# Attention core rebuilt: a 32x32 chunk recurrence, a half-size inversion, other batch groups, and a mixture summed on TensorE

## The reference, cut to what matters

```python
attn = where(strict_lower, -(kb @ k.T), 0)        # 32x32 per chunk, kb = k * beta
T = inv(eye - attn);  u = T @ (v * beta);  w = T @ kb
for each chunk:                                    # S is 32x32
    u_i = u - w @ S
    o_i = q @ S + where(lower, q @ k.T, 0) @ u_i
    S = S + k.T @ u_i
```

## Time and profile before

| | |
|---|---|
| median of 3 runs | 506.85 us (506.24 to 511.7) |
| the profiled execution | 506.55 us, of which the span of its instructions is 504.8 us |
| PE busy | 400.6 us (79%), 2822 matmuls, 2822 weight loads |
| DVE, ACT, POOL busy | 343.4 us (68%), 311.7 us (62%), 43.1 us (9%) |
| mean granted TensorE clock | 0.874 of full speed |
| DMA queue of instruction refills (q8) | 34 packets, 0.56 MB |

### The profile page before, as it was taken

How to read it: one execution, slowest core, us unless ns; L and a number is a source line. 1 busy time by engine, 2 the same in 40 slices (tenths; PEclk the granted TensorE clock), 3 DMA queues, 4 the chain that set the end, 5 groups by cost and what they waited for, 6 DMA issues and landing times. The chain is left out here.

```text
span 504.8 us, 7248 instructions
## 1 busy us (share of the span) xinstructions
PE 400.6 (79%) x2822; PEld 290.1 (57%) x2822; DVE 343.4 (68%) x532; ACT 311.7 (62%) x471; POOL 43.1 (9%) x44
## 2 busy tenths in 40 slices
PE   5469998999889958898279999729523298899994
PEld 2346775678667647787146766615201286576783
DVE  2893479747138569999956866694986987487532
ACT  4866886797465757875246646373334179668862
POOL 3000000000000001000400000000719500000000
PEclk9789999999999976799759978658958599999998
DMA  8700007300000000015600000000000000001001
GB/s 281 245 3 1 3 0 213 82 3 0 1 1 1 0 3 1 3 45 148 224 6 2 1 1 1 1 1 0 0 0 1 0 3 1 1 0 45 3 1 42
DMA packets 13484, 17.24 MB, mean 34 GB/s; under 512 B 896, under 2 KB 9088, under 8 KB 13440
## 3 DMA queue, kind: packets, MB, share of 16 engines
q1 hardware_dynamic: 13296, 16.58, 10.7%
q10 hardware_dynamic: 144, 0.01, 0.0%
HBM read 15.55 MB, written 1.05 MB: 33 GB/s over the span
## 5 line engine op out<-in xcount | busy, mean ns | idle before, releaser
L711 PE MATMUL ps_a<-acts,w_f 128*128 128x512 f32 x256 | 104.5, 408 | 1.4 <-DVE acts L1093 0.9
L712 PE MATMUL ps_a<-acts,w_f 128*128 128x512 f32 x256 | 101.4, 396 | 0.0
L711 PEld LDWEIGHTS ps_a<-acts,w_f 128*128 128x128 f32 x256 | 49.1, 192 | 15.2 <-ACT acts L573 1.7
L712 PEld LDWEIGHTS ps_a<-acts,w_f 128*128 128x128 f32 x256 | 49.1, 192 | 11.5 <-issue 1.4
L573 ACT ACTIVATE acts<-ps_a,vec 128x512 fp32r<-128x512 f32 x64 | 44.5, 695 | 0.0
L846 PE MATMUL ps_a<-xnp,conv_w 128*128 128x512 f32 x156 | 38.1, 402 | 0.0
L1112 DVE TENSOR_TENSOR acts<-ghbuf,acts 128x512 fp32r<-128x512 f32 x32 | 21.6, 690 | 23.4 <-ACT acts L573 23.1
L1112 DVE TENSOR_TENSOR acts<-gbuf,acts 128x512 fp32r<-128x512 f32 x32 | 21.7, 690 | 22.3 <-ACT acts L573 22.3
L711 PE MATMUL ps_a<-xn,w_f 128*128 128x512 f32 x32 | 15.0, 470 | 25.3 <-DVE ln L1001 22.2
L846 PEld LDWEIGHTS ps_a<-xnp,conv_w 128*128 128x128 f32 x156 | 29.3, 188 | 8.2 <-issue 1.4
L755 PE MATMUL ps_a<-arena 128*128 128x32 f32 x128 | 17.7, 296 | 12.4 <-ACT arena L482 12.4
(11 more groups left out here) (202 smaller groups left out, 855.2 us busy)
## 6 DMA issues: line engine op xcount, KB each, us to landing
toep<-in_fir SPq DMA_DIRECT2D x16, 288.0 KB, 5.0
w_in<-in_h SPq DMA_DIRECT2D x4, 1024.0 KB, 8.0
g_rows<-in_gW SPq DMA_DIRECT2D x4, 640.0 KB, 6.8
w_in<-in_w SPq DMA_DIRECT2D x6, 256.0 KB, 4.2
iobuf<-in_x SPq DMA_DIRECT2D x4, 256.0 KB, 6.5
toep<-in_taps SPq DMA_DIRECT2D x1, 768.0 KB, 6.7
y<-iobuf SPq DMA_DIRECT2D x12, 64.0 KB
toep<-in_proj SPq DMA_DIRECT2D x1, 256.0 KB, 9.1
```

The costliest lines, as they stand in the source:

```text
L711: e.matmul(bank, w, hi, start=start, stop=False)
L712: return e.matmul(bank, w, lo, start=False, stop=stop)
```

## The change

The inversion is now of the two 16x16 diagonal blocks of all matrices of both groups at once: 15 steps, each over four blocks a partition. `gram` 1 is put ahead of it. The part below the diagonal is applied on PE: `yy` multiplies the block-diagonal inverse with [v, k] (side by side, 64 columns), `zz` multiplies by the lower left block, DVE subtracts, and `uu` multiplies with the inverse again. `aq` and `bo` then form, for every chunk, batch and head, the 32x32 matrices of S' = A·S + B and o = Q·S + O, and `rec` runs the recurrence with them: per chunk and group 32 products of 32x32x32 on PE and one add of 256 columns on DVE. The block-diagonal operands, `spread_u`, `mask_s`, `blocks` and `plain_u` are gone. All products of `yy` to `rec` are 32x32 in the stationary operand; in `yy`, `zz`, `uu` and `rec` successive products use row group and column group with the same number, in `aq` and `bo` one row group and the four column groups. The counts are, over both groups: `yy`, `zz`, `uu` 256 products each, `aq` 224, `bo` 512, `rec` 416.

`token` comes before `window`. The sums of path 4 stand ahead of `fir`; six sums stand between the chunks, those of path 3 at the end. A "half" of a path is now four batches, not half of each row of tokens; tiles of x are contiguous, and the store is one DMA a tile. POOL's program loses the block fills and the mixture and gets `masked`. The mixture is one multiply on DVE for a group, and `addmix` sums the five paths as products with the identity on PE (ten 128x128x512 fp32 products a group); the one of group 1 stands in the second FFN, after the means and ahead of the variances. `refine` does with three operations what took four. The rounding copy of the second FFN's weights (`round`) is behind both square roots of the statistics. Buffers are laid out anew.

```diff
+    s += [("addmix", 2, 1)] if last else []
...
-    s += [("sumsq", 2, NT - 1), ("gram", 2, 0), ("inverse", 2, 0)]
+    s += [("sumsq", 2, NT - 1), ("gram", 2, 0), ("gram", 2, 1), ("inverse", 2, 0)]
+    s += [("token", 2, i) for i in range(12)]
     s += [("window", 2, i) for i in range(16)]
-    s += [("gram", 2, 1), ("inverse", 2, 1)]
-    s += [("token", 2, i) for i in range(12)]
+    s += [("turn4", 2, 0)] + [("stat", 2, q) for q in range(2)]
     s += [("fir", 2, i) for i in range(16)]
-    s += [("chain", 2, n) for n in range(NCH)]
-    s += [("stats", 2, 0)]
-    for half in range(2):
-        s += [("gate", 2, 2 * half + i) for i in range(2)] + [("logit", 2, 2 * half + i) for i in range(2)]
-        s += [("soft", 2, 0), ("mix", 2, 0)] if half == 0 else []
-    s += [("scale", 2, 0), ("soft", 2, 1), ("wo", 2, 0), ("wo", 2, 1)]
+    for kind in ("yy", "zz", "uu", "aq", "bo"):
+        s += [(kind, 2, g) for g in range(G)]
+    for n in range(1, NCH):
+        s += [("rec", 2, G * n + g) for g in range(G)]
+        s += [("stat", 2, n + 1)] if n < 7 else []
+    s += [("turn3", 2, g) for g in range(G)]
+    s += [("stat", 2, q) for q in (8, 9)]
+    s += [("turn", 2, g) for g in range(G)] + [("round", 2, 0)]
+    s += [("gate", 2, i) for i in range(2)] + [("logit", 2, i) for i in range(2)]
+    s += [("soft", 2, 0), ("mix", 2, 0)]
+    s += [("gate", 2, i) for i in (2, 3)] + [("logit", 2, i) for i in (2, 3)]
+    s += [("addmix", 2, 0), ("soft", 2, 1), ("mix", 2, 1), ("scale", 2, 0), ("wo", 2, 0), ("wo", 2, 1)]
...
+STATS = ((4, 0), (4, 1), (0, 0), (1, 0), (2, 0), (0, 1), (1, 1), (2, 1), (3, 0), (3, 1))
...
+                own(e.memset(alt[:, g, :, :, 0, 0:HB].rearrange("p h n t -> p (h n) t"), 0.0))
+                below = alt[:, g, :, :, 0, HB:DH].rearrange("p h n t -> p (h n) t")
+                e.tensor_scalar(below, below, mask[:, 0, HB:HB + 1], None, ALU.mult).then_inc(S["masked"], 1)
+            e.wait_ge(S["path4"], G)
+            e.wait_ge(S["pe_a"], A_AT[("window", 2, 15)] + 1)
             e.memset(at("st", 2048), 0.0).then_inc(S["st_zero"], 1)
...
+                elif kind in ("yy", "uu"):
+                    for h in range(H):
+                        e.wait_ge(S["pe_a"], a + h + 1)
+                        e.activation(yu[:, i, h].rearrange("p n c -> p (n c)"), ps_a[(a + h) % NRING][:, :], ACT.Copy
...
+                elif kind == "turn":
+                    e.wait_ge(S["dve_stat"], LAST_STAT[i] + 1)
+                    e.activation(st[:, i, :, 3:4 * P:4], st[:, i, :, 1:4 * P:4], ACT.Sqrt).then_inc(S["act_norm"], 1)
+                elif kind == "round":
+                    e.wait_ge(S["ld_w2"], 32)
+                    e.wait_ge(S["ld_h2"], 48)
+                    e.activation(w_f[1][:, :], w_in[1][:, 0:5632], ACT.Copy).then_inc(S["w2_round"], 1)
...
+                elif kind in ("yy", "uu"):
+                    if kind == "yy":
+                        e.wait_ge(S["inv_done"], i + 1)
+                        e.wait_ge(S["act_a"], A_AT[("token", 2, 11)] + 1)
+                    for h in range(H):
+                        if kind == "uu":
+                            e.wait_ge(S["dve_d"], D_AT[("zz", 2, i)] + h + 1)
+                        bank = take_a(a + h)
+                        for n in range(NCH):
+                            for b in range(4):
+                                r = slice(32 * b, 32 * b + 32)
+                                last = e.matmul(bank[r, 64 * n:64 * n + 64], xt[r, i, h, n],
+                                                vk[r, i, h, n].rearrange("p x c -> p (x c)"), start=True, stop=True)
+                        last.then_inc(S["pe_a"], 1)
+                elif kind == "zz":
...
+                        bank = take_d(dd + h)
+                        for n in range(NCH):
+                            for b in range(4):
+                                r = slice(32 * b, 32 * b + 32)
+                                last = e.matmul(bank[r, 64 * n:64 * n + 64], alt[r, i, h, n, 0], yu[r, i, h, n],
...
+                        last.then_inc(S["pe_d"], 1)
...
+                elif kind == "aq":
+                    e.wait_ge(S["act_a"], A_AT[("uu", 2, i)] + H)
+                    for b in range(4):
+                        bank, r = take_d(dd + b), slice(32 * b, 32 * b + 32)
+                        for n in range(1, NCH):
                             for h in range(H):
                                 c = slice(32 * h, 32 * h + 32)
...
+                                last = e.matmul(bank[c, 64 * n:64 * n + 64], yu[r, i, h, n, DH:2 * DH],
+                                                alt[r, i, h, n, 1:3].rearrange("p x c -> p (x c)"), start=True, stop=True)
+                        last.then_inc(S["pe_d"], 1)
...
+                elif kind == "bo":
+                    for b in range(4):
+                        bank, r = take_a(a + b)[:, :], slice(32 * b, 32 * b + 32)
+                        for n in range(NCH):
+                            for h in range(H):
+                                c, o = slice(32 * h, 32 * h + 32), 64 * n
+                                e.matmul(bank[c, o:o + DH], alt[r, i, h, n, 2], yu[r, i, h, n, 0:DH],
+                                         start=True, stop=True)
+                                last = e.matmul(bank[c, o + DH:o + 2 * DH], yu[r, i, h, n, 0:DH], alt[r, i, h, n, 1],
+                                                start=True, stop=True)
+                        last.then_inc(S["pe_a"], 1)
...
+                elif kind == "rec":
+                    n, g = i // G, i % G
+                    if n == 1:
+                        e.wait_ge(S["act_a"], A_AT[("bo", 2, g)] + 4)
+                        e.wait_ge(S["dve_d"], D_AT[("aq", 2, g)] + 4)
                     else:
...
+                        e.wait_ge(S["dve_d"], D_AT[("rec", 2, i - G)] + 1)
+                    bank = take_d(dd)
+                    for part in ((0, 1) if n < NCH - 1 else (1,)):
+                        for b in range(4):
+                            for h in range(H):
+                                r, o = slice(32 * h, 32 * h + 32), 128 * part + 32 * b
+                                state, step = bo[r, g, n - 1, 0, b], aqs[g][r, b, n]
+                                last = e.matmul(bank[r, o:o + DH], *((step[:, 1], state), (state, step[:, 0]))[part],
+                                                start=True, stop=True)
+                    last.then_inc(S["pe_d"], 1)
...
+                        bank = take_a(a + k)[:, :].rearrange("p (t c) -> p t c", c=DH)
+                        for p in range(P):
+                            last = e.matmul(bank, ident[:, :], paths[p][:, i, HB * k:HB * k + HB],
+                                            start=p == 0, stop=p == P - 1)
+                        last.then_inc(S["pe_a"], 1)
...
+                for o, h, v in zip(out, shape(half_y2), shape(src)):
+                    own(e.scalar_tensor_tensor(out=o, in0=h, scalar=1.5, in1=v, op0=ALU.subtract, op1=ALU.mult))
...
+                p, g = STATS[q]
+                own(e.tensor_reduce(st[:, g, :, 4 * p], paths[p][:, g], AX_X, ALU.add))
+                own(e.tensor_reduce(st[:, g, :, 4 * p + 2], paths[p][:, g], AX_X, ALU.add, apply_absolute_value=True))
                 e.wait_ge(S["act_stat"], q + 1)
-                e.tensor_reduce(st[:, r, 4 * p + 1], sq_p[:, q % 2], AX_X, ALU.add).then_inc(S["dve_stat"], 1)
+                e.tensor_reduce(st[:, g, :, 4 * p + 1], sq_p[SQ_SLOT[q]], AX_X, ALU.add).then_inc(S["dve_stat"], 1)
...
+                        k = HB - 1 - j
+                        shape = [128, 2 * G, k, j + 1]
+                        sub = halves_t[:, :, j + 1:HB, 0:j + 1]
+                        prod = tmp[:, 0:2 * G * k * (j + 1)].rearrange("p (a i c) -> p a i c", a=2 * G, i=k)
+                        own(e.tensor_tensor(prod, halves_l[:, :, j + 1:HB, j:j + 1].to_broadcast(shape),
+                                            halves_t[:, :, j:j + 1, 0:j + 1].to_broadcast(shape), ALU.mult))
                         settle()
                         own(e.tensor_tensor(sub, sub, prod, ALU.subtract))
...
+                        rhs = vk[:, i, h].rearrange("p n x c -> p (n x c)")
+                        e.tensor_tensor(rhs, rhs, ps_d[:, (dd + h) % NRING], ALU.subtract).then_inc(S["dve_d"], 1)
...
+                        own(e.tensor_tensor(aqs[i][:, b, 1:NCH, 1], eye[:, :].unsqueeze(1).to_broadcast([128, NCH - 1, DH]),
+                                            src[:, :, 1], ALU.subtract))
+                        e.tensor_tensor(aqs[i][:, b, 1:NCH, 0], kq[:, 1, NCH * i + 1:NCH * i + NCH, 32 * b:32 * b + 32],
+                                        src[:, :, 0], ALU.subtract).then_inc(S["dve_d"], 1)
...
+                    r = slice(0 if n < NCH - 1 else 128, 256)
+                    dst = bo[:, g, n].rearrange("p x b c -> p (x b c)")[:, r]
+                    if n == 1:
```

(43 more changed lines are left out.)

500 lines of the change are left out of this document (169 added, 331 removed).

## The result

| | before | after |
|---|---|---|
| median | 506.55 us (505.96 to 511.70, 4 runs) | 546.74 us (545.85 to 547.75, 4 runs) |
| span of the profiled execution | 504.8 us | 544.5 us |
| mean granted clock | 0.874 | 0.858 |
| PE busy, DVE busy | 400.6, 343.4 us | 413.9, 291.1 us |
| refills (q8) | 34 packets, 0.56 MB | 59 packets, 0.97 MB |

What follows compares the result with a forecast made beforehand. The new core was taken as bound by refills of PE's instructions. 504.8 + 41 (to the gate) + 3 (to the second FFN) - 3 (rest) = 545.8 us span, 547.6 with 1.75 around it, taken as 548; own range 535 to 562, eight in ten 518 to 578.

Steps and rivals of the forecast that it cites:

- Up to the first `yy`: Everything up to the end of the filters: the new core's first product starts near 251 us, where the chain started at 254.8.
- the step on the filters: Before the filters: ACT can't go on, since `squares(1)` stands ahead of `fir` and waits for sums; free at 231.5 us.
- The new core on PE: `yy` to `bo`: 3,008 pairs, 23.5 instruction blocks at 3.75 us each, 86 us; bounds 38 and 94 us.
- The recurrence: `rec`: DVE's work is longer than PE's, 4.35 us a chunk, 29 us in all; bounds 22 and 40.
- To the gate: From the end of `rec` at 366: DVE's transposes, six sums and waits, 12.8 us; gate at 379, +41.
- Gate to second FFN: From the gate to the second FFN's first `up`: 65 us against 62.1 before, +3, with 12 for `addmix` 1.
- two logits, softmax 1 (4.6): Between gate and second FFN, after the first mixture's multiply: two logits 1.5 us and softmax 1 4.6 us.
- The rest: Last store in one piece -2 us, `refine` in both FFNs -1 us; everything else in the FFNs stands.
- instructions never late: Rival on the new core: 12.5 ns a pair, 38 instead of 86 us, 500 us in all; chance 0.08.
- half way: Rival on the new core: refills partly overlap, 13 to 16 ns a pair, 502 to 512 us; chance 0.06.
- The third: Rival on the new core: PE at half clock throughout, 26 ns a pair, 78 us, 540 in all; chance 0.12.
- The fourth: Rival on `yy`, `zz`, `uu`: diagonal blocks exclude each other, 50 ns a pair, 582 us in all; chance 0.08.

Runs made afterwards that it cites:

- experiment 5: Kernel after, with the sums of paths 0 to 2 taken behind `yy`, `zz` and `uu` instead of between the chunks of `rec`: 544.59 us.
- Experiment 8: Kernel after, with softmax 1 ahead of mixture 0's sums and `addmix` 1 behind both variances of the second FFN: 534.22 us.
- experiment 1: Kernel after, with products of `yy`, `zz`, `uu` and `aq` moving 32 columns instead of 64, same instruction count: 545.17 us.
- experiment 3: Kernel after, with products of `yy`, `zz`, `uu`, `aq` and `bo` in bf16, each issued twice: 548.14 us.
- experiment 6: Kernel after, with the second FFN's weights loaded behind the last copy of `bo` instead of behind the last filter: 545.08 us.
- experiment 2: Kernel after, with products of `yy`, `zz`, `uu`, `aq` and `bo` in bf16, one pair each instead of two: 502.43 us.

## Why the prediction was right

Point by point, the forecast and the trace of the kernel after:

- **Up to the first `yy`**: forecast 251, found 245.24. The inversion's 30 operations took 11.85 us, forecast 11.8, and ACT stood behind `squares(1)` for 6.34 us, as the step on the filters said. From ACT's release to the first `yy` it was 19.3 us, forecast 19.5. The 5.8 us are sizes: the norms ended at 188.1, not 191 (the attention itself began 2.4 us earlier than before, and which of the small edits in the first FFN gave that was not tried); the step from the sums to ACT's release took 1.0 and not 1.7; `gram` 1 took 6.36 us, not 7.6, behind a wait of 0.95; POOL beside the inversion cost one operation of 0.61 us instead of 0.32, where I had given 1.5.
- **The new core on PE**: forecast 86, found 90.3 to the first product of `rec`. The price of 3.75 us a block held (3.8 on average without the first distance). What was missing is the second FFN's load, which lies on the first two blocks: one pause of 4.91 us where all others are 0.3 to 2.0. Both kernels start it behind the last filter, but before the change the chain behind that point had 615 pairs in 68.6 us, and no refill started between 236.6 and 255.8, while the load ran from 243.4 to 253.7.
- **The recurrence**: forecast 29, found 28.1, at 4.04 us a chunk against 4.35: the two adds take 0.66 us together, not 0.94. DVE stood without a pause there, so the bound lay in it; that the refill's pace lies as high is what experiment 5 showed.
- **To the gate**: forecast 12.8, found 12.4. The gate started at 376.1, 38.1 us later than before, forecast 41.
- **Gate to second FFN**: forecast 65, found 67.7. Two terms were wrong, in opposite directions. `addmix` 1 took 8.75 us, at full clock, and not 12. And the step "two logits, softmax 1 (4.6)" did not look at ACT's order, where the exponential stands behind copies that wait for PE: 7.6 us of waiting, forecast none beyond the usual 0.4. Experiment 8 gave it back. No slow layer norm was there, as forecast: before the change DVE's operation at L1005 took 4.71 us beside POOL and 0.42 us at the median of its eight, and without POOL beside it the layer norm's operations after the change took 0.43 to 0.69.
- **The rest**: forecast 101.8 (545.8 - 379 - 65), found 100.7.

The sum missed by 1.3 us, with errors of -5.8, +4.3, -0.9, -0.4, +2.7 and -1.1 in its terms (the rest is rounding); the mechanism was right, and part of the total's accuracy is luck.

Of the rivals, the first two (instructions never late, half way) had 38 to 48 us for the stretch. The third (half clock sets the pace) fell in experiments 1 and 3: at a mean clock of 0.69 or 0.53 the stretch is the same. It was nearest to the truth in single blocks of 64 columns at half clock, where the pause was as short as 0.33 us. The fourth (blocks on the diagonal exclude each other) had 50 ns a pair; `yy` shows 129 pairs in 2.02 us, 15.7 ns, or about 14 without the last one's own length, where `gram` has 12.5. In `yy`, `zz`, `uu` and `rec` successive products of different row groups write one bank, in `yy` 0.23 us long each and about 14 ns apart, and the trace shows no price above 2 ns a pair against the earlier trace rows, both at a granted clock of 1.00. The size of a block, which the forecast took from one pass of `gram`, held: 254 or 256 instructions between two pauses, and 16 KB in every packet of q8. The refills were not hidden: PE stands idle for 35.7 of the stretch's 90.6 us, 0.3 to 2.0 us in nearly every block.

## What to carry to other kernels

Count instructions, not only work. The stretch of this kernel issues 3,008 pairs of 32x32 products with nothing between them, at 14 to 16 ns a pair where PE ran at full clock, and its price was the number of instruction blocks (254 to 256 instructions) times the distance of two refills, 3.6 to 3.8 us on average in these kernels. Busy shares, clock and width said nothing on it (90.6, 89.2 and 90.2 us with 55, 45 and 39 us of work); look for "issue" in the engine's timeline at equal counts. Then fewer instructions are the cure to try (one pair a product instead of two took the stretch from 90.6 to 42.9 us), a bulk load is better put where no refill is due (83.4 us without it), and a step moved to another engine must be followed through each engine's order, since it drags its copies in front of what stood there (7.6 us of waiting for the exponential).

## What the runs showed of the hardware that was not expected

- A bulk load delayed refills where it was put beside them. At 247.62 us PE had gone on, and the next refill started 4.6 us later, where 1.0 to 1.7 is usual in this kernel; the distance became 6.9 us. Beside the load behind `bo` (experiment 6) there were pauses of 3.10 and 4.75 us. Between `yy` and `bo`, where PE waited neither beside a load nor for another engine, distances were 3.2 to 4.6 us and pauses at most 2.7 in all kernels.
- The pace of refills was the same with another clock and with another kind of product. Without the first distance they were 3.79 us apart on average in the stretch of the kernel after (mean clock 0.69, fp32), 3.75 in experiment 1 (0.53, fp32, half the columns), 3.68 in experiment 2 (0.59, bf16) and 3.82 in experiment 3 (0.53, bf16).
- Diagonal 32x32 products of four row groups in turn, all into one bank, ran at about 14 ns a pair at a granted clock of 1.00 (`yy`, 129 pairs in 2.02 us), nearly the 12.5 of the earlier trace rows.
- The ten 128x128x512 products with the identity that sum five paths took 8.85 and 8.75 us for the two groups in fp32 and 2.53 and 2.88 in fp32r.
